# Attention kernel: maximum tiles from half-precision q and k, a block's context in one PSUM bank, six of eight low parts on GpSimd

## The reference

```python
x = x + layernorm(attention_block(layernorm(x)))   # x: (2, 2048, 256) fp32
x = x + layernorm(ffn(layernorm(x)))
# attention_block: 16 heads of 64
q, k, v = x @ Wq + bq, x @ Wk + bk, x @ Wv + bv
attn = softmax(q @ k.T / 8)                         # per head, 2048 x 2048
y = x + (attn @ v) @ Wo + bo;  return layernorm(y, eps=1e-3) * gamma + beta
# ffn: silu(x @ wg.T) * (x @ wu.T) @ wd.T, hidden 768, integer weights / 127
```

## Time and profile before

| what | us |
|---|---|
| median of 3 runs (lowest, highest) | 3343.22 (3339.74, 3346.07) |
| profiled execution, its own time | 3347.19 |
| its span, first to last instruction | 3345.4 |
| PE busy | 3095.9 (93%) |
| PEld busy | 2475.0 (74%) |
| DVE busy | 2784.4 (83%) |
| ACT busy | 2473.8 (74%) |
| POOL busy | 2016.6 (60%) |

### The profile page before, as it was taken

How to read it: one execution, slowest core, us unless ns; L and a number is a source line. 1 busy time by engine, 2 the same in 40 slices (tenths; PEclk the granted TensorE clock), 3 DMA queues, 4 the chain that set the end, 5 groups by cost and what they waited for, 6 DMA issues and landing times. The chain is left out here.

```text
span 3345.4 us, 77779 instructions
## 1 busy us (share of the span) xinstructions
PE 3095.9 (93%) x25440; PEld 2475.0 (74%) x25440; DVE 2784.4 (83%) x4983; ACT 2473.8 (74%) x4715; POOL 2016.6 (60%) x1550
## 2 busy tenths in 40 slices
PE   5899999999999999969999999999999999878897
PEld 4677777777777777757777777777777778667775
DVE  5688988888888888976888888888888889578886
ACT  3688888888888788856888787878888889733222
POOL 3577767676667666636777666766667677512232
PEclk9999999999999999989999999999999999989998
DMA  3522222222222122115122222222222222221110
GB/s 106 136 53 53 54 54 54 54 54 54 54 48 57 43 55 56 42 31 172 33 56 57 42 56 46 54 54 54 54 54 54 54 53 52 96 83 51 63 44 19
DMA packets 206585, 197.39 MB, mean 59 GB/s; under 512 B 157648, under 2 KB 180304, under 8 KB 193872
## 3 DMA queue, kind: packets, MB, share of 16 engines
q1 hardware_dynamic: 206160, 192.00, 24.7%
HBM read 53.16 MB, written 37.88 MB: 27 GB/s over the span
## 5 line engine op out<-in xcount | busy, mean ns | idle before, releaser
L442 POOL TENSOR_TENSOR p_l<-p_f,p_h 128x512 f16<-128x512 f32 x1280 | 1627.0, 1293 | 546.9 <-ACT p_h L514 546.1
L562 DVE TENSOR_REDUCE mx<-ps_aux 128x1 f32<-128x512 f32 x2048 | 1384.5, 684 | 289.3 <-PE ps_aux L735 258.8
L513 ACT ACTIVATE p_f<-ps_score 128x512 f32<-128x512 f32 x2048 | 1272.2, 622 | 358.7 <-PE ps_score L746 337.3
L514 ACT ACTIVATE p_h<-ps_score 128x512 f16<-128x512 f32 x2048 | 1283.0, 628 | 0.0
L735 PE MATMUL ps_aux<-k_hihi,q_hilo 128*128 128x512 f32 x2048 | 1037.5, 507 | 93.8 <-DVE mx L562 44.4
L768 PE MATMUL ps_ctx<-v_hi_one_lo,p_h 128*128 128x129 f16 x8192 | 929.2, 223 | 2.3 <-POOL p_l L442 1.5
L768 PEld LDWEIGHTS ps_ctx<-v_hi_one_lo,p_h 128*128 128x128 f16 x8192 | 609.2, 99 | 322.2 <-issue 264.2
L746 PE MATMUL ps_score<-q_hi_max,k_lo_one 65*128 65x512 f32 x2048 | 826.5, 404 | 0.0
L745 PE MATMUL ps_score<-q_hilo,k_hihi 128*128 128x512 f32 x2048 | 821.2, 401 | 3.7 <-DMA q_hi_max<-negm 3.1
L768 PE MATMUL ps_ctx<-v_hi_one_lo,p_l 128*128 128x65 f16 x8192 | 783.3, 195 | 0.0
L735 PEld LDWEIGHTS ps_aux<-k_hihi,q_hilo 128*128 128x128 f32 x2048 | 632.3, 309 | 173.1 <-DVE mx L562 69.1
(11 more groups left out here) (122 smaller groups left out, 2538.4 us busy)
## 6 DMA issues: line engine op xcount, KB each, us to landing
k_hihi<-hi_st SPq DMA_DIRECT2D x64, 512.0 KB, 8.6
v_heads<-v_new SPq DMA_DIRECT2D x64, 258.0 KB, 2.0
v_hi_one_lo<-v_heads SPq DMA_DIRECT2D x32, 516.0 KB, 9.7
q_hilo<-hi_st SPq DMA_DIRECT2D x32, 512.0 KB, 4.4
q_hilo<-lo_st SPq DMA_DIRECT2D x32, 512.0 KB, 6.6
q_hi_max<-hi_st SPq DMA_DIRECT2D x32, 512.0 KB, 9.2
k_lo_one<-lo_st SPq DMA_DIRECT2D x32, 512.0 KB, 10.1
heads<-ctx_n SPq DMA_DIRECT2D x128, 128.0 KB, 2.0
```

What stands on the lines that cost most here:

```text
L442: nc.gpsimd.tensor_tensor(p_l[:, r], p_f[:, r], p_h[:, r], ALU.subtract).then_inc(lo_pool, 1)
L513: nc.scalar.activation(p_f[:, r], ps_score[:, bank], ACT.Exp, scale=K ** -0.5)
L514: nc.scalar.activation(p_h[:, r], ps_score[:, bank], ACT.Exp, scale=K ** -0.5).then_inc(exp_done, 1)
L562: nc.vector.reduce_max(mx[:, blk % 2, tt, ch:ch + 1], ps_aux[:, bank], AX_X).then_inc(max_read, 1)
```

## The change

- **Maximum tiles.** New fp16 tiles `qM` and `kM` (`q_half`, `k_half`), 64 rows of q and k and a 65th row of zeros, take the place of `qA` and `kA` in `max_tile`. VectorE makes them with one more copy per chunk (`half_st`), SyncE fills them with two more DMAs per head (8 in place of 6). The streamed columns stay 512.
- **Weighing.** High and low values now add into the same 64 columns: V is scaled by 16 instead of its low part by 2048 (and the ones are 16), so three matmuls per 128 queries take the place of two: `p_h` with 65 columns, `p_h` with 64, `p_l` with 65. A block's context is 260 columns of one bank, and the blocks take turns in the two banks of `ps_ctx`.
- **End of a block.** ScalarE's copy and VectorE's addition go; VectorE takes reciprocals and divides straight from PSUM, at `kt` 4.
- **Low parts.** VectorE subtracts at `t % 4 == 1` (two of eight), GpSimd the other six.
- **Projection.** A chunk now stands ahead of both weighings of its pair.
- **Prologue.** The bias of the values is scaled by 16 once per batch, and the addition of the bias scales the product too.

```diff
 def lo_on_dve(t):
-    return t % 8 in (1, 3, 5)
+    return t % 4 == 1
...
+        qM = [sb(f"q_half{u}", [K + 1, S], F16) for u in range(2)]
+        kM = [sb(f"k_half{u}", [K + 1, S], F16) for u in range(2)]
...
+                sp.wait_ge(half_ready, (g + 1) * NB + 1)
+                for dst, src in ((qM[u][0:K], half_st[0:K]), (kM[u][0:K], half_st[K:P])):
+                    sp.dma_start(dst, src).then_inc(slot_full, 16)
...
-            def copy_sums(nb):
-                act.wait_ge(pv_done, (nb + 1) * KT + PROBS)
-                act.wait_ge(ev_step, nb * 2 + 2)
-                nc.scalar.activation(sums[:, :, :], ps_ctx[:, :, 0:2 * VW], ACT.Copy).then_inc(ctx_free, 1)
...
                 nc.vector.tensor_copy(hi_w[:, cols], qk_new[:, :]).then_inc(hi_ready, 1)
+                nc.vector.tensor_copy(half_st[:, cols], qk_new[:, :]).then_inc(half_ready, 1)
...
+            def divide(j, nb):
+                acc = ps_ctx[:, j % 2, 0:TB * (K + 1)].rearrange("p (t c) -> p t c", c=K + 1)
+                dve.wait_ge(pv_done, (nb + 1) * KT + PROBS)
                 nc.vector.reciprocal(rden[:, :], acc[:, :, K]).then_inc(ev_step, 1)
...
-                nc.vector.tensor_tensor(ctx_n[:, j % 2], ctx_u[:, :, :],
+                nc.vector.tensor_tensor(ctx_n[:, j % 2], acc[:, :, 0:K],
...
-                q = qA[u][:, blk * BLK:(blk + 1) * BLK].rearrange("k (p t) -> k t p", t=TB)[:, tt]
-                nc.tensor.matmul(ps_aux[:, bank], q, kA[u][:, ch * BLK:(ch + 1) * BLK],
+                q = qM[u][:, blk * BLK:(blk + 1) * BLK].rearrange("k (p t) -> k t p", t=TB)[:, tt]
+                nc.tensor.matmul(ps_aux[:, bank], q, kM[u][:, ch * BLK:(ch + 1) * BLK],
...
                 for q in range(TB):
-                    acc = ps_ctx[:, q // 2, (q % 2) * VW:(q % 2 + 1) * VW]
-                    parts = [(p_h, VW), (p_l, K + 1)]
-                    if q % 2:
-                        parts.reverse()
-                    for p, width in parts:
-                        mm = nc.tensor.matmul(acc[:, 0:width], p[:, r, q * P:(q + 1) * P], V[u][:, kt, 0:width],
...
+                    acc = ps_ctx[:, j % 2, q * (K + 1):(q + 1) * (K + 1)]
+                    toks = slice(q * P, (q + 1) * P)
+                    v_one, v_lo = V[u][:, kt, 0:K + 1], V[u][:, kt, K + 1:VW]
+                    nc.tensor.matmul(acc, p_h[:, r, toks], v_one, start=(kt == 0 and q == 0), stop=False,
+                                     skip_group_check=True)
+                    nc.tensor.matmul(acc[:, 0:K], p_h[:, r, toks], v_lo, start=False, stop=False,
+                                     skip_group_check=True)
+                    mm = nc.tensor.matmul(acc, p_l[:, r, toks], v_one, start=False,
+                                          stop=(kt == KT - 1 and q == TB - 1), skip_group_check=True)
...
                     if t % 2:
-                        weigh(u, g, t - 1)
                         for chunk, number in chunks[t]:
                             project(g + u + 2, chunk, number % 2)
+                        weigh(u, g, t - 1)
                         weigh(u, g, t)
```

More of the change, by code:

```diff
@@ L35 @@
 P_SHIFT = 5.545177444479562
-LO_SCALE = 2048.0
-SUMS_AT = 4
+V_SCALE = 16.0
+DIVIDE_AT = 4
 CHUNKS_AT = (3, 9)
+FILLS = 8
 def lo_on_dve(t):
-    return t % 8 in (1, 3, 5)
+    return t % 4 == 1
 def lo_counts(t):
@@ L191, in attention @@
         bv_in = sem("bv_in")
+        bv_scaled = sem("bv_scaled")
         vh_ready = sem("vh_ready")
@@ L203, in attention @@
         hi_ready = sem("hi_ready")
+        half_ready = sem("half_ready")
         staged = sem("staged")
@@ L417, in _ @@
                 nc.gpsimd.memset(kB[u][K:K + 1, :].bitcast(F32), 1.0).then_inc(ones_set, 1)
-                pool.wait_ge(ones_set, u + 1)
+                nc.gpsimd.memset(qM[u][K:K + 1, :], 0.0).then_inc(ones_set, 1)
+                nc.gpsimd.memset(kM[u][K:K + 1, :], 0.0).then_inc(ones_set, 1)
+                pool.wait_ge(ones_set, 3 * u + 3)
             def low_chunk(g, chunk):
@@ L464, in take_chunk @@
                 act.wait_ge(staged, g * NB + chunk + 1)
+                act.wait_ge(half_ready, g * NB + chunk + 1)
                 act.wait_ge(aux_full, n + 1)
@@ L520, in head @@
                             .then_inc(xh_ready, 1)
[L521 to L524, removed]
                 return n
@@ L532, in _ @@
             dve.sem_inc(max_read, 2)
-            dve.sem_inc(ev_step, 2)
+            dve.sem_inc(half_ready, 1)
+            dve.sem_inc(ctx_free, 2)
             dve.sem_inc(w_split, 1)
-            nc.vector.memset(v_new[:, :, :, K:K + 1], 1.0)
+            nc.vector.memset(v_new[:, :, :, K:K + 1], V_SCALE)
             dve.wait_ge(const_in, 32)
@@ L579, in low @@
                     nc.vector.tensor_tensor(p_l[:, r], p_f[:, r], p_h[:, r], ALU.subtract).then_inc(lo_dve, 1)
[L581 to L586, removed]
+            def divide(j, nb):
+                acc = ps_ctx[:, j % 2, 0:TB * (K + 1)].rearrange("p (t c) -> p t c", c=K + 1)
+                dve.wait_ge(pv_done, (nb + 1) * KT + PROBS)
                 nc.vector.reciprocal(rden[:, :], acc[:, :, K]).then_inc(ev_step, 1)
-            def divide(j, nb):
-                dve.wait_ge(ev_step, nb * 2 + 4)
+                dve.wait_ge(ev_step, nb + 1)
                 dve.wait_ge(ctx_out[j % 2], (nb - j) * 8 + j // 2 * 16 + 16)
-                nc.vector.tensor_tensor(ctx_n[:, j % 2], ctx_u[:, :, :],
+                nc.vector.tensor_tensor(ctx_n[:, j % 2], acc[:, :, 0:K],
                                         rden[:, :].unsqueeze(2).to_broadcast([P, TB, K]), ALU.mult)\
-                    .then_inc(ctx_ready, 1)
+                    .then_inc(ctx_free, 1)
             def norm_part(b, k, part):
@@ L625, in low_weights @@
                     dve.wait_ge(bv_in, b * 16 + 16)
+                    nc.vector.tensor_scalar(bv_all, bv_all, V_SCALE, None, ALU.mult).then_inc(bv_scaled, 1)
+                    dve.wait_ge(bv_scaled, b + 1)
                 def norm_group(k):
@@ L646, in prologue @@
                             dve.wait_ge(v_ready, b * KT * 2 + a - 3)
-                        nc.vector.tensor_tensor(p_f[:, 2 + a % 4], ps_score[:, m % RING],
-                                                bv_all[:, half * BLK:(half + 1) * BLK], ALU.add).then_inc(pro_free, 1)
+                        nc.vector.scalar_tensor_tensor(out=p_f[:, 2 + a % 4], in0=ps_score[:, m % RING], scalar=V_SCALE,
+                                                       in1=bv_all[:, half * BLK:(half + 1) * BLK], op0=ALU.mult,
+                                                       op1=ALU.add).then_inc(pro_free, 1)
                         if a == 2 * KT - 12:
@@ L679, in head @@
                     block_before = not (first and u == 0 and j == 0)
-                    if kt == 2 and block_before:
-                        add_sums((g + u) * NB + j - 1)
-                    if kt == 4 and block_before:
+                    if kt == DIVIDE_AT and block_before:
                         divide((j - 1) % NB, (g + u) * NB + j - 1)
@@ L704, in _ @@
             pe.wait_ge(const_in, 32)
-            pe.wait_ge(ones_set, 2)
+            pe.wait_ge(ones_set, 6)
             used = []
```

20 lines of the change are left out of this document (6 added, 14 removed).

## The result

The change made the kernel slower by half a per cent, little but clear of the noise: 3358.06 us median of 10 runs (3345.50 to 3375.12) against 3343.81 us before, a ratio of 1.0049 with a 95% interval of 1.0029 to 1.007. Forecast were 3215 us, 143 us less, in a range of 3130 to 3300. The profiled execution took 3368.91 us.

A forecast was written before the change was run, and what follows sets the result against it. TensorE was taken as the bound, VectorE close behind. Terms -218 + 0 + 57 - 10 - 3 + 0 + 40 + 5 = -129 us on 3347.19 gave 3218, stated as 3215 us, range 3130 to 3300.

The forecast's parts named there:

- What bounds the kernel: Whole kernel: TensorE sets the pace, 2.30 us per pair of steps, VectorE close behind at 96% in a head's first half.
- first maximum tile: First maximum tile of each pair on TensorE: fp16 weights cut 0.43 to 0.217 us, saving 218 us (200 to 230).
- weighing: Weighing matmuls on TensorE, 24 slots per pair: 0.746 us where 0.69 stood, costing 57 us in total.
- Rivals C and D: TensorE: C, weighings bound by slower weight loads, 3497 us, chance 0.07; D, maximum tiles no faster, 3414 to 3432, 0.04.
- Second maximum tile: Second maximum tile of each pair on TensorE: faster columns and a later weight load cancel, 0 us (-15 to +30).
- chunks: 112 projection chunks in the heads, moved ahead of the first weighing: 0.085 us less each, saving 10 us.
- ScalarE: ScalarE's copy of 614 ns goes 128 times; TensorE hardly waited for it, saving 3 us.
- Prologues and slots: Head DMAs and batch starts: two more DMAs per head stay hidden; they and the scaled bias lie open at batch starts, +5 us.
- VectorE: VectorE's low parts, additions and copies: net relief of 284 us, share near 96% in the first half, waits unchanged, 0 us.
- GpSimd, +40: TensorE's waits on GpSimd, with 256 more low parts, and on the chunk's bank: +40 us (0 to +120).
- Rival A: GpSimd becomes the bound as its and VectorE's low parts block each other in steps with chunks: 3273 to 3300 us, chance 0.24.
- The sum: Whole kernel: all terms add to -129 us on the profiled 3347.19, giving 3218, stated as 3215 us; chance 0.50.

The follow-up runs named there:

- rows first: Changed kernel with SyncE's order altered: half-precision fills and `w_raw` first, then the row of maxima, then six fp32 fills and V; 3213.5 us, ratio 0.9616.
- seven of eight: Rows first with ScalarE making the half-precision copy, VectorE subtracting one of eight low parts, GpSimd the others; 3249.02 us, ratio 0.9701.

## Why the prediction was wrong

- *What bounds the kernel; first maximum tile; weighing.* Right, in sizes too: 2.15 us per pair for 2.14, 0.75 for 0.746, though the maximum tile's own time shows only in a sum with the score matmul. Rivals C and D are out.
- *Second maximum tile, chunks, ScalarE.* Within what can be told. The chunk's 10 us could not be found (3214.65 against 3213.5).
- *Prologues and slots: "Two more DMAs per head hide behind half a head."* This step failed. I looked at who needs the half-precision tiles, half a head later, and not at what stands behind their DMAs on SyncE: the row of maxima and `w_raw`. What stood at nothing in the sum measured 145 us: 59 us of stall, most of 112 us of lower clock and 19 us by way of `w_raw`, by estimates that overlap. The +5 us for the prologues themselves came true: TensorE's wait there for the last fill went from 9.8 to 15.1 us. One order changed gives them back and lands at 3213.5, for 3215 forecast.
- *VectorE: "a net relief of 284 us ... its waits stay: 0".* Wrong in size. TensorE's weight loads waited 118 us for its maxima after the change, and 102 with rows first, where 65 stood. Its share did not stay near 96%: with rows first it is busy 14.96 of 17.50 us in a quarter without chunks (85%). Plain busy time is no measure of it. Its low parts grew from 928 ns to 1091 ns each, and a copy of 0.42 us cost 0.9 or 0.1 (14 us over 112 chunks) in the kernel before, by its place.
- *GpSimd, +40.* Its waits went from 56 to 72 us, and to 92 with rows first, so the size holds. Rival A did not happen at six of eight; the loss at seven of eight points its way.
- *The sum.* That rows first lands 2 us from the forecast is in part luck. Between the kernel before and it, TensorE's busy time fell by 138 us (3095.9 to 2958.2), where maximum tiles, weighing and chunks were to save 171. Its idle time grew by 2 us (249.5 to 251.8), where waits and prologues were to add some 40. Two misses of 30 to 40 us cancel; of the first, some 21 us are more time at the lower clock (250 us for 207, half of it lost).
- *"The loop edges and the feed-forward part stay."* True but for the clock: I priced no stall with the lower clock that follows it.
- No rival had the queue in it, though the margin could have been read. Before, the row is issued at 1086.29 and is wanted by the first score matmul of block 2:

```profile
1091.60 0.39 PE L745 MATMUL ps_score<-q_hilo,k_hihi 128*128 128x512 f32 x1
```

How long it takes from issue to landing depends on what else is under way. The eight rows of two heads have a median of 2.2 us (first line); the one behind the fills took 3.0 (second line, 1085 to 1088 us), and 3.2 after the change (third line, 1095.5 to 1099 us):

```profile
q_hi_max<-negm SPq DMA_DIRECT2D x8, 2.0 KB, 2.2
q_hi_max<-negm SPq DMA_DIRECT2D x1, 2.0 KB, 3.0
q_hi_max<-negm SPq DMA_DIRECT2D x1, 2.0 KB, 3.2
```

Counted from the first fill, the row landed after 20.6 us (17.6 + 3.0) and was wanted after 22.9, so 2.3 us were to spare. After the change it landed after 23.3 (20.1 + 3.2) and was wanted after 21.4, since the steps are 0.075 us shorter. That is 1.9 us too late, and TensorE started 2.03 us late. The two fills alone take 3.5 us in a full queue (2.02 and 1.50); the DMA of V, 2.05 us before and 0.64 now, gives part of it back.

## What to carry to other kernels

A DMA that nobody needs for long still stands ahead of one that somebody needs soon: when one is added, list what is queued behind it and how much margin that had, after the speed-up itself has shortened it. Put small, urgent transfers ahead of bulk fills. Where VectorE's and GpSimd's subtractions from SBUF meet, look at which starts first after each handover. Exchanging two lines was worth 85 us in the kernel before with the copies added; with rows first, taking the copy off VectorE altogether was worth 6. So measure it in the kernel at hand.

## What the runs showed of the hardware

- With SyncE's queue full (eight fills and V ahead), the time of an issue belongs to its place: `w_raw` 4.67 us behind the fills, and the 2 KB row 4.45 when it took that place.
- A stall of TensorE of about 2 us per head was followed by the lower clock behind 27 of 28 such waits: 431 us at it with them, 250 without. By the clock these stalls cost 90 us (half of 181, an estimate) on top of their 59.
- VectorE's and GpSimd's subtractions from SBUF hardly overlap: 0.68 and 1.67 us if VectorE starts first, 1.78 and 1.40 if GpSimd does.
